# Waiting on GpSimd for the last four scatter-adds at the end of a fused cross-attention and mixture-of-experts kernel

## The chip, the cores and the metric

The kernel runs on one core of one Trainium2 chip. The metric is device time in microseconds (us): the time of one execution of the whole kernel. Three executions were timed before the change.

## The reference, cut to what matters

The kernel computes one decoder layer over 2048 rows of 256 numbers: self-attention, cross-attention over 1601 context rows, a dense feed-forward block, and then a mixture-of-experts block, which is the part that runs last:

```
router_logits = x @ wg.T                        # 8 experts
probs = softmax(router_logits)
topk_w, topk_idx = top_k(probs, 2)              # each row goes to two experts
topk_w = topk_w / sum(topk_w)
h1 = einsum('th,eih->tei', x, w1)
h3 = einsum('th,eih->tei', x, w3)
y = einsum('tei,ehi->teh', silu(h1) * h3, w2)
out = einsum('te,teh->th', expert_w, y)         # sum over the row's two experts
x = x + out
```

## The kernel before, in words

Five engines run a program each, written out by hand in one block: SyncE (SP), GpSimd (POOL), ScalarE (ACT), TensorE (PE) and VectorE (DVE). They order each other by counting semaphores alone. Up to about 350 us the kernel does the attention and dense parts; the rest is the expert part.

In the expert part the rows are sorted by expert into NJ = 39 tiles of 128 places. Tile n passes through a ring of RING = 4 buffers (slot n % 4):

- GpSimd gathers the tile's rows from the scratch tensor `hrow` by an indirect DMA (`gather`, line 899).
- PE multiplies with the expert's up-weights, ACT and DVE apply silu and the product (`e_sil`, `e_act`), SP turns the result by a DMA transpose (`act_turn`, line 658; for the last tile PE turns it instead), and PE multiplies with the down-weights.
- ACT or DVE scales the result by the gate and writes it to `ys` (`weighted`, DVE line 2208), which raises `e_y`.
- GpSimd adds the tile's 128 rows into the output tensor `out` in HBM by an indirect DMA with accumulation (`add`, line 925), called scatter-add below. When it has landed it raises the semaphore `e_add0` to `e_add3` of its slot by 16.

Each row of `out` gets two such additions, from two experts, so two scatter-adds that could meet the same row must not be in flight together. `add(n)` therefore waits on GpSimd for the landing of earlier scatter-adds (`add_done`, or a wait against a number read from a table), and issues a tiny multiplication into `gap` (line 923) ahead of the DMA. The waits of `add(38)`, the last one, are for scatter-adds 35, 36 and 37 or earlier ones, and then for `e_y` of tile 38.

GpSimd's program ends with `add(NJ - 1)`. SP's program ends with a wait for the landing of every scatter-add:

```
for s in range(RING):
    wait(sp, f"e_add{s}", 16 * len(range(s, NJ, RING)))
```

Of the kernel before, what the change touches and what calls it, by code (L numbers as in the profile page):

```python
# [61 lines left out]
NJ = (TOP * S + NE * (P - 1)) // P  # L62
# [7 lines left out]
RING, AHEAD, BEHIND = 4, 6, 3  # L70
# [8 lines left out]
def xattn_ffn_moe(nc, x, z, zT, w1, w2, wgT, we, b1, rows, out):  # L79
    with ExitStack() as ctx:  # L80
# [262 lines left out]
        def wait(eng, name, n):  # L343
            eng.wait_ge(sm[name], n)
# [119 lines left out]
        NG = len(GROUPS)  # L464
        LAG = 2
        LAST_OF = [max(n for n, (j, _) in enumerate(GROUPS) if j == b) for b in range(NB)]

        def width_of(parts):
            return sum((TB - t0) * P for _, t0, _ in parts)
# [209 lines left out]
        def _(pool):  # L679
# [148 lines left out]
            def weigh(j):  # L828

                b = slice(j * TB, (j + 1) * TB)  # L830
                wait(pool, "r_exp", j + 1)
                link(g.tensor_scalar(den[:], ex[:], 1.0, 1.0 / GS, ALU.add, ALU.mult))
                link(g.tensor_tensor(gf[:, :, 0], den[:], minus, ALU.pow))
                link(g.tensor_tensor(gf[:, :, 1], ex[:], gf[:, :, 0], ALU.mult))
                link(g.tensor_copy(vals[:, 1, b, :], gf))
                g.tensor_tensor(vals[:, 2, b, :], gf, vals[:, 1, b, :], ALU.subtract).then_inc(sm["r_val"], 1)
# [48 lines left out]
            def phase_of(n):  # L885
                return [p for p, (_, n0, n1) in enumerate(PHASES) if n0 <= n < n1][0]

            def rows_of(p):

                return PHASES[p][0] * TB * P if p < 2 else S + SPARE * P  # L890
# [11 lines left out]
            def add_done(n):  # L902
                wait(pool, f"e_add{n % RING}", 16 * (n // RING + 1))

            def add(n):

                p = phase_of(n)
                wait(pool, "x1_out", 16 * TB * PHASES[p][0])
                alone = n <= RING or n == PHASES[p][1]
                if n > 2:  # L910
                    add_done(n - 3)
                if n > 1 and (alone or n % RING == 1):
                    add_done(n - 2)
                if n and alone:
                    add_done(n - 1)
                if not alone:
                    if n == PHASES[p][1] + 1 or n == RING + 1:
                        wait(pool, "r_next", p + 1)
                    done = pool.value_load(before[0:1, n:n + 1], min_val=16, max_val=16 * NJ)
                    pool.wait_ge(sm[f"e_add{(n - 1) % RING}"], done)  # L920
                    if n % RING != 1:
                        pool.wait_ge(sm[f"e_add{(n - 2) % RING}"], done)
                    g.tensor_tensor(gap[:, n:n + 1], expo[:, 0:1], expo[:, 0:1], ALU.mult)
                wait(pool, "e_y", n + 1)
                g.indirect_dma_start(out[:rows_of(p), :], bass.IndirectOffsetOnAxis(ridx[:, n:n + 1], 0),  # L925
                                     ys[:, n % RING, :], None, compute_op=ALU.add
                                     ).then_inc(sm[f"e_add{n % RING}"], 16)
# [10 lines left out]
            for n in range(NJ):  # L938
# [7 lines left out]
                if n == LOGITS_AT - 2:  # L946
                    gates(NB - 1)
                    weigh(NB - 1)
            add(NJ - 1)

        @block.scalar
# [636 lines left out]
        def _(dve):  # L1589
# [397 lines left out]
            def tiles_hot(p):  # L1987

                _, n0, n1 = PHASES[p]
                k, n = pairs_of(p), n1 - n0  # L1990
                dve.wait_ge(sm["c_pv"], NT)
                link(v.scalar_tensor_tensor(hot_tiles(p), tkey[:, n0:n1].unsqueeze(1).broadcast_to([P, k, n]), float(P),
                                            keys.rearrange("p t c -> p (t c)")[:, :k].unsqueeze(2).broadcast_to([P, k, n]),
                                            ALU.mult, ALU.is_equal))
# [330 lines left out]
```

## Time and profile before

| what | value |
|---|---|
| device time, three runs | 554.15, 549.77, 547.66 us; median 549.77 us |
| span of the profiled execution | 546.3 us |
| busy share of the span: PE, DVE, ACT, POOL | 91%, 69%, 53%, 54% |
| instructions | 11105 |

The profiled execution has no device time of its own in the list. Its span, from the start of its first instruction to the end of its last, is 1.4 us under the fastest of the three runs and 3.5 us under their median. What lies between span and device time is outside the program's instructions. All rows below count time from the first instruction of that execution. A "q" behind an engine's name (POOLq, SPq) means its sequencer, the part that executes waits, branches and DRAINs and hands the rest to the engine. These do not count as busy.

### The profile page before, as it was taken

The page shows a single profiled execution, that of the slowest core. Times are in us where ns is not written, and L with a number is a line of the kernel's source. Part 1 is how long each engine was busy: PE and PEld are TensorE (multiplying, and loading weights), DVE is VectorE, ACT ScalarE, POOL GpSimd, SP SyncE. Part 2 cuts the span into 40 slices and gives each one's busy share as a digit, 9 for nine tenths or more (in the row PEclk, how much of TensorE's full clock was granted, in tenths as well). Part 3 has the DMA queues.
Part 4 walks back from the last instruction along what each step waited for, and adds up shares of the span by engine and source line. Part 5 has one row for each costly group of instructions (what it writes and reads, how often), then busy time and mean ns, then how long its engine had stood idle before and what let it go on. Part 6 is the DMA issues. An engine that isn't in the chain of part 4 may idle for free.

```text
span 546.3 us, 11105 instructions
## 1 busy us (share of the span) xinstructions
PE 499.1 (91%) x3721; PEld 329.5 (60%) x3721; DVE 377.8 (69%) x974; ACT 287.0 (53%) x588; POOL 295.8 (54%) x332
## 2 busy tenths in 40 slices
PE   3999999989999999799999988689997999999992
PEld 1676766655666675567565667444564656656661
DVE  5899886588777678868876887987866544444441
ACT  2747867564749446764457384474553333433430
POOL 3564121005553339735895759643647576777753
PEclk9999999999999999999999999999998999999997
DMA  8020624348895367863779553125796668887973
GB/s 273 8 71 26 193 69 131 92 83 144 154 162 133 97 112 142 172 155 90 117 181 193 155 92 108 54 71 109 139 161 93 94 123 133 133 134 127 135 109 39
DMA packets 135315, 65.62 MB, mean 120 GB/s; under 512 B 109757, under 2 KB 126590, under 8 KB 135262
## 3 DMA queue, kind: packets, MB, share of 16 engines
q1 hardware_dynamic: 127774, 54.69, 46.9%
q0 software_dynamic: 7488, 10.23, 12.4%
q8 instruction: 32, 0.52, 0.4%
q14 instruction: 21, 0.17, 0.1%
HBM read 28.19 MB, written 10.35 MB: 71 GB/s over the span
## 4 chain that ended last, share of the span: by engine, by line
PE 49%; DVE 15%; ACT 10%; POOL 9%; DMA 9%; issue 6%; POOLq 1%; SPq 0%; DVEq 0%; ACTq 0%
PE ps L1154 38%; DMA out<-y,qst 4%; ACT ps L971 3%; PE ps L1236 3%; PE ps L1238 3%; PE ps L1237 3%; POOL y L813 3%; ACT prob L970 3%; DVE cmax L1658 2%; DMA probT<-prob 2%; POOL y L846 1%; DMA y<-hrow,qst 1%; POOL rstd L806 1%; PE ps L1433 1%; DVE tT L1867 1%
## 5 line engine op out<-in xcount | busy, mean ns | idle before, releaser
L1154 PE MATMUL ps<-arena,probT 128*128 128x256 f16 (+2 forms) x1092 | 181.7, 319 | 5.6 <-DMA probT<-prob 3.1
L1154 PEld LDWEIGHTS ps<-arena,probT 128*128 128x128 f16 (+1 forms) x1092 | 104.9, 98 | 65.2 <-issue 11.8
L970 ACT ACTIVATE prob<-ps,nbias 128x512 f16<-128x512 f32 x64 | 39.0, 610 | 76.7 <-DVE nbias L1664 76.7
L925 POOL DMA_INDIRECT out<-y,qst x39 | 62.5, 1603 | 28.2 <-ACT y L1120 9.7
L1154 PE MATMUL ps<-arena,qT 128*128 128x512 f16 (+1 forms) x384 | 69.2, 332 | 3.1 <-DVE prob L1799 3.0
L2194 DVE SCALAR_TENSOR_TENSOR ps<-ps,w1m 128x512 f32<-128x512 f32 x39 | 27.3, 699 | 54.5 <-ACT w1m L1097 52.3
L1097 ACT ACTIVATE w1m<-ps 128x512 f32<-128x512 f32 x39 | 23.3, 597 | 76.3 <-PE ps L1154 61.5
L1154 PE MATMUL ps<-arena,tT 128*128 x468 | 57.9, 274 | 0.8 <-DVE tT L2289 0.6
L1154 PEld LDWEIGHTS ps<-arena,qT 128*128 128x128 f16 x384 | 32.5, 97 | 37.8 <-issue 4.2
L1799 DVE TENSOR_TENSOR prob<-ps,prob 128x512 f16<-128x512 f32 x64 | 36.3, 573 | 25.6 <-ACT ps L971 25.5
L1154 PE MATMUL ps<-tT 128*128 128x512 f16 (+3 forms) x240 | 51.8, 355 | 1.8 <-DVE tT L1626 1.8
L1154 PE MATMUL ps<-w2s,tT 128*128 128x256 f16 x384 | 48.2, 273 | 5.4 <-DVE tT L1867 5.1
L1154 PEld LDWEIGHTS ps<-arena,tT 128*128 128x128 f16 x468 | 44.1, 98 | 6.4 <-issue 1.3
L1154 PE MATMUL ps<-probT,w1m 128*128 128x512 f16 (+1 forms) x192 | 44.1, 326 | 3.5 <-DVE tT L1867 1.7
L899 POOL DMA_INDIRECT y<-hrow,qst x39 | 39.7, 1019 | 12.1 <-issue 11.2
L1154 PEld LDWEIGHTS ps<-w2s,tT 128*128 128x128 f16 x384 | 36.5, 98 | 15.9 <-issue 4.4
L989 ACT ACTIVATE probT<-ps,shift 128x512 f16<-128x512 f32 (+1 forms) x36 | 23.9, 664 | 31.9 <-PE ps L1154 21.0
L743 POOL TENSOR_TENSOR rstd<-veps,expo 128x1 f32<-128x1 f32 x16 | 10.0, 623 | 56.3 <-DVE veps L1693 56.3
L756 POOL TENSOR_TENSOR srstd<-sveps,expo 128x4 f32<-128x4 f32 x4 | 4.3, 1086 | 65.1 <-DVE sveps L1756 65.1
L1236 PE MATMUL ps<-arena,probT 128*128 128x257 f16 x136 | 37.2, 274 | 0.9 <-DVE probT L1726 0.5
L971 ACT ACTIVATE ps<-ps,nbias 128x512 f32<-128x512 f32 x64 | 37.5, 586 | 0.0
L1238 PE MATMUL ps<-arena,probT 128*128 128x257 f16 x136 | 37.1, 273 | 0.0
(214 smaller groups left out, 958.1 us busy)
## 6 DMA issues: line engine op xcount, KB each, us to landing
stage<-we_in SPq DMA_DIRECT2D x33, 256.0 KB, 3.2
prob<-we_in SPq DMA_DIRECT2D x15, 256.0 KB, 3.0
xin<-x_in SPq DMA_DIRECT2D x16, 128.0 KB, 2.8
out<-y SPq DMA_DIRECT2D x16, 128.0 KB
hrow<-tT SPq DMA_DIRECT2D x4, 512.0 KB, 4.7
y<-x_in SPq DMA_DIRECT2D x3, 512.0 KB, 6.5
stage<-z_in SPq DMA_DIRECT2D x4, 256.0 KB, 5.2
prob<-w_in SPq DMA_DIRECT2D x4, 256.0 KB, 3.0
```

The source lines that it names most:

```text
L813: g.tensor_scalar(blk(j)[:, m, :], blk(j)[:, m, :], mv4[:, m, 0:1], rstd4[:, m:m + 1], ALU.subtract, ALU.mult).then_inc(sm["n_nrm"], 1)
L899: g.indirect_dma_start(xg[:, n % RING, :], None, hrow[:rows_of(p), :], bass.IndirectOffsetOnAxis(ridx[:, n:n + 1], 0)).then_inc(sm[f"e_x{n ...
L925: g.indirect_dma_start(out[:rows_of(p), :], bass.IndirectOffsetOnAxis(ridx[:, n:n + 1], 0), ys[:, n % RING, :], None, compute_op=ALU.add). ...
L970: a.activation(row_cols(q, 0, c), ps[c][:, :w], ACT.Exp, bias=nbias[:, q, :], scale=SM)
L971: a.activation(ps[c][:, :w], ps[c][:, :w], ACT.Exp, bias=nbias[:, q, :], scale=SM, accum_out=esum[:, q, c:c + 1]).then_inc(sm["c_exp"], 1)
L989: a.activation(p16[:, s % 4, 0, :w], ps[s % 2][:, :w], ACT.Exp, bias=shift[:], scale=SM).then_inc(sm["s_exp"], 1)
L1097: a.activation(sil[:, q, :], ps[2 * q][:], ACT.Silu, scale=1.0 / WS).then_inc(sm["e_sil"], 1)
L1154: r = t.matmul(o, lhs(a), rhs(b), start=first and n == 0, stop=last and n == 2)
L1236: t.matmul(o[:, :D + 1], hi, yvh[:, kt, :D + 1], start=kt == 0, stop=False)
L1238: r = t.matmul(o[:, :D + 1], lo, yvh[:, kt, :D + 1], start=False, stop=last)
L1799: v.tensor_tensor(row_cols(q, 1, c), ps[c][:, :w], row_cols(q, 0, c), ALU.subtract).then_inc(sm["c_lo"], 1)
L2194: v.scalar_tensor_tensor(ps[2 * q + 1][:], ps[2 * q + 1][:], 1.0 / WS, sil[:, q, :], ALU.mult, ALU.mult).then_inc(sm["e_act"], 1)
```

## The change

Two lines are added behind the last `add` of GpSimd's program. NJ - RING is 35, so GpSimd waits for the landing of scatter-adds 35, 36, 37 and 38: `e_add3` at 144 and `e_add0`, `e_add1`, `e_add2` at 160. These are the four values that SP waits for already.

```
@@ -947,6 +947,8 @@
                     gates(NB - 1)
                     weigh(NB - 1)
             add(NJ - 1)
+            for n in range(NJ - RING, NJ):
+                add_done(n)
 
 
         @block.scalar
```

No computation and no DMA is added, removed or moved. The last rows of GpSimd's program before the change, from the last scatter-add to the branch into the end of the block (`qst` holds the table of row numbers, `ys` lies in `y`):

```order
L923 TENSOR_TENSOR gap<-expo 128x1 [waits e_add0]
L925 DMA out<-y,qst 2560x256 [waits e_y]
L919 TENSOR_LOAD qst [waits e_add3,x1_out]
L919 ISA x2
L923 TENSOR_TENSOR gap<-expo 128x1 [waits e_add0,e_add1]
L925 DMA out<-y,qst 2560x256 [waits e_y]
L80 UNCONDITIONAL_BRANCH
```

And after it, the same place of GpSimd's program:

```order
L919 TENSOR_LOAD qst [waits e_add3,x1_out]
L919 ISA x2
L923 TENSOR_TENSOR gap<-expo 128x1 [waits e_add0,e_add1]
L925 DMA out<-y,qst 2560x256 [waits e_y]
L80 UNCONDITIONAL_BRANCH [waits e_add1,e_add2,e_add0,e_add3]
```

Only the branch at the end differs: it now stands behind the four landings. The DRAIN of GpSimd comes after the branch in both. SP's program ends with the same waits in both:

```order
L565 DMA hrow<-tT 128x4x512 [waits m_hlo]
L658 DMA_TRANSPOSE tT<-prob 128x8x128 [waits e_alo,e_down] x29
L80 UNCONDITIONAL_BRANCH [waits e_add2,e_add3,e_add1,e_add0]
```

## Rows read from the trace of the kernel before

**Rows 1.** Windows view, last 14 us: busy time by engine, granted clock, DMA share, GB/s

```profile
core 0: us, PE busy (x) PEld busy (x) DVE busy (x) ACT busy (x) POOL busy (x), PEclk, DMA share, GB/s
532.00:539.60 7.60, 4.28 (x40) 3.17 (x37) 3.16 (x6) 1.32 (x3) 5.18 (x6) 0.99 0.55 60
539.60:541.90 2.30, 0.00 (x0) 0.00 (x0) 0.00 (x0) 0.00 (x0) 0.00 (x0) 0.50 0.55 57
541.90:546.30 4.40, 0.00 (x0) 0.00 (x0) 0.00 (x0) 0.00 (x0) 0.00 (x0) 0.50 0.01 2
```

**Rows 2.** Chain that ended last, stretch 526 to 547 us: start, length, what

```profile
526.28 6.54 PE ps L1154 x48
532.84 0.49 DVE y L2208
533.34 0.27 issue
533.61 3.47 DMA out<-y,qst
537.12 0.76 POOL gap L923
537.88 1.71 POOLq L80
```

**Rows 3.** Timeline of POOL, 525 to 547 us

```profile
525.79 0.18 POOL L923 TENSOR_TENSOR gap<-expo 128x1 f32<-128x1 f32 x1 [4.09 <-DMA out<-y,qst]
...
536.11 1.55 POOL L925 DMA_INDIRECT out<-y,qst  x1 [0.69 <-DVE y L2208]
537.12 0.76 POOL L923 TENSOR_TENSOR gap<-expo 128x1 f32<-128x1 f32 x1
538.04 1.55 POOL L925 DMA_INDIRECT out<-y,qst  x1 [0.16 <-issue]
```

**Rows 4.** Source view, line 80, the end of the block: ns min/median/max, first and last start

```profile
L80 POOLq EVENT_SEMAPHORE  x2: 17/17/17, 546.1 to 546.2; - x2
L80 ACTq DRAIN  x1: 626/626/626, 534.8 to 534.8; - x1
L80 PEldq DRAIN  x1: 638/638/638, 536.5 to 536.5; - x1
L80 DVEq DRAIN  x1: 524/524/524, 537.2 to 537.2; - x1
L80 POOLq DRAIN  x1: 8357/8357/8357, 537.7 to 537.7; - x1
L80 SPq COMPARE_BRANCH  x1: 41/41/41, 542.3 to 542.3; - x1
L80 SPq DRAIN  x1: 7/7/7, 542.5 to 542.5; - x1
```

**Rows 5.** Source view, line 344 (semaphore waits) on SP, 500 us to the end

```profile
L344 SPq EVENT_SEMAPHORE  x9: 17/17/28, 504.1 to 541.9; - x9
```

**Rows 6.** Waits of SP's queue, 515 us to the end: total, times, longest

```profile
SPq L344 <- DMA out<-y,qst: 11.7, 1, 11.7
...
SPq L80 <- PEq L80: 3.8, 1, 3.8
```

**Rows 7.** Source view, line 2318, the first instructions of the program

```profile
L2318 SPq DRAIN  x1: 7/7/7, 0.0 to 0.0; - x1
...
L2318 POOLq DRAIN  x1: 174/174/174, 0.4 to 0.4; - x1
L2318 POOL MEMSET const-uint8-127<- x1: 97/97/97, 0.4 to 0.4; 128x1 uint8 x1
```

More of the change, by code:

```diff
@@ L949, in _ @@
             add(NJ - 1)
+            for n in range(NJ - RING, NJ):
+                add_done(n)
         @block.scalar
```

## The prediction

> **What bounds the kernel now.** The change touches the last few microseconds alone, so I first split the end of the span by windows [rows 1]. Up to 539.6 us there is work on every engine. From there on no engine is busy. For 2.3 us the DMA engines still move data (share 0.55, 57 GB/s), and in the last 4.4 us they move almost nothing (share 0.01, 2 GB/s). So the program's last 4.4 us pass with neither computing nor transfer. The question is who holds the end of the span in that time.
>
> The chain that ended last [rows 2] goes PE, the scaling on DVE, a scatter-add that another one had to wait for (3.47 us), the `gap` multiplication, and then POOLq L80, GpSimd's sequencer at the end of the block. In that view its last piece is only 1.71 us long and begins at 537.88, which leaves the rest of the span unexplained. So I read the single instructions of line 80 [rows 4]. Five DRAINs stand there. ACT's, PE's and DVE's start between 534.8 and 537.2 and are done by 537.7. SP's starts at 542.5 and takes 7 ns. GpSimd's starts at 537.7 and takes 8357 ns, to 537.7 + 8.36 = 546.0 us. Its two semaphore instructions follow at 546.1 and 546.2, and the span ends at 546.3. **GpSimd's DRAIN ends last**, not SP's wait for the landings: SP reaches the meeting at 542.5 and sits there for 3.8 us [rows 6]. That wait is put down to PEq, but PE's DRAIN was over at 537.2; the engine that came last is GpSimd.
>
> What the DRAIN covers can be cut into three stretches:
> - 537.7 to 539.6: GpSimd's own last scatter-add, which starts at 538.04 and takes 1.55 us [rows 3]. The sequencer is ahead of its engine here, so the DRAIN is already begun while this instruction runs.
> - 539.6 to 541.9: the rows are landing. The last semaphore wait of SP is through at 541.9 [rows 5], so the last scatter-add takes 541.9 - 538.0 = 3.9 us from its start to its landing, near the 3.47 us that the chain shows for an earlier one [rows 2].
> - 541.9 to 546.0: 4.1 us in which the profile shows nothing that the DRAIN could wait for.
>
> From the end of the scatter-add's issue to the end of the DRAIN it is 546.0 - 539.6 = 6.4 us. From the end of the DRAIN to the end of the span it is 546.3 - 546.0 = 0.3 us, the meeting itself.
>
> **The change part by part.** It adds four waits ahead of GpSimd's branch and nothing else. On GpSimd only the branch, the DRAIN and the meeting are queued behind them, and who waits for these is all four other engines, which are idle by then. No gather or add is behind the waits, so nothing ahead of 539.6 us moves: the tiles, the transposes and the landings come as before. The waits themselves end at 541.9, as SP's equal ones do. The instructions cost 17 to 28 ns each [rows 5], and they lie in the time in which the rows land: nothing until 541.9. SP then needs from 541.9 to 542.5, 0.6 us, for what is left of its waits, its branch and the start of its DRAIN [rows 4, 5]. GpSimd's branch ran before under cover of its last scatter-add, and now it stands in the open as SP's does. So GpSimd's DRAIN should start at 541.9 + 0.6 = 542.5 instead of 537.7, 4.8 us later.
>
> All now hangs on how long a DRAIN of GpSimd takes that starts 0.6 us behind the last landing. No row of before shows that. The trace bounds it from both sides:
> - Short end: the DRAIN at the program's start takes 174 ns, and most of that is a MEMSET still running on the engine (97 ns, started beside it) [rows 7]. No scatter-add had gone out by then. With 0.17 us the span would end at 542.5 + 0.2 + 0.3 = 543.0: a change of -3.3 us.
> - Long end: the whole 8.36 us again, end at 542.5 + 8.4 + 0.3 = 551.2: +4.9 us. But 1.9 us of it (537.7 to 539.6) were the engine's own scatter-add, which is done by then; without them it is 6.4 us and an end at 549.2: +2.9 us.
> - Between them: if only the 4.1 us behind the landing are the DRAIN's own, they either run from the landing however the DRAIN starts (end as before, 0), or they start with the DRAIN (542.5 + 4.1 + 0.3 = 546.9, +0.6 us).
>
> I take the middle case, at the mean of its two ends, **+0.3 us**. The reason: the two DRAINs of GpSimd that the trace has differ in one thing above all, that the gathers and scatter-adds of 39 tiles stand between them, and the long one outlasts the last landing by 4.1 us. If it only waited for landings, as SP does, it would be over at 541.9 and not at 546.0. So it does something of its own that takes 4.1 us and comes with having issued such DMAs, and a wait for a semaphore on the sequencer does not do that work for it. Whether the work can run before the DRAIN asks for it is what splits 0 from +0.6.
>
> A rule of the Trainium skill speaks for another outcome. "VectorE: DVE Perf Modes", in the section "The DRAIN you can't avoid", says that the DRAINs which frame a kernel take a constant 12 ns or so on all five engines. The trace agrees for SP, at either end of the program (7 ns), and disagrees for GpSimd, with 174 and 8357 ns [rows 4, 7]. By that rule the whole length would be waiting, the DRAIN behind the new waits would be as short as SP's, and the end would come at 542.5 + 0.3 = 542.8, or -3.5 us. It is the first rival below, which is priced from the rows alone.
>
> **The sum.** Against the profiled execution: span 546.3 + 0.0 (everything ahead of 539.6) + 0.0 (the waits, under the landing) + 0.3 (the DRAIN) = 546.6 us. This execution lies 3.5 us under the median of the three runs, 549.77, so the forecast in device time is 549.8 + 0.3 = 550.1 us. The three runs are 6.5 us apart (1.2%), more than any case here is worth. About 1%, or 5.5 us, is what a measurement of this kernel can tell from no change.
>
> **The rivals.**
> - *The DRAIN was waiting for transfers, and finds none now.* Then it looks for finished transfers slowly or with long pauses while some are open, and the 4.1 us are that lateness. With nothing open it is as short as at the start of the program: -3.3 us, 546.5 us. For it: the 174 ns of [rows 7]. Against it: the DRAIN at the start had no DMA of GpSimd behind it at all, so it does not tell "all landed" from "none issued". Chance 0.25.
> - *The DRAIN costs a fixed time from its start on an idle engine.* Then 6.4 us that ran from 539.6, partly under the landing, now run from 542.5, wholly in the open: +2.9 us, 552.7 us. This is the rival on the other side: the change takes away an overlap. Its place is the DRAIN of GpSimd, its price 542.5 - 539.6 = 2.9 us, and it decides as soon as the DRAIN's own work does not depend on the landing. For it: nothing in the profile ties the DRAIN's end at 546.0 to the landing at 541.9 rather than to the issue's end at 539.6. Against it: only that a DRAIN of 6.4 us without any waiting is the longer guess. The extreme of it, 8.4 us from the start, gives +4.9 us, 554.7 us. Chance 0.2 and 0.03.
> - *The change does nothing that can be seen*, because SP waits for the same landings already and GpSimd would have met it at the block's end anyway. Without reading line 80 this is the natural reading; it gives 0 too, but it needs GpSimd's DRAIN to be off the path, and [rows 4] show that it is on it. Its time is part of the forecast's case.
>
> **How the numbers follow.** Forecast case, 0 to +0.6 us: 0.5 (its own range 549.8 to 550.4 us, before the scatter of runs). Short DRAIN: 0.25. Fixed DRAIN: 0.2, its extreme 0.03. The remaining 0.02 is for a change elsewhere in the program. The range runs from the short DRAIN's 546.5 less a little scatter, 545.8, to the fixed DRAIN's 552.7 and a little above, 553.0. No case is worth 1%: the largest likely ones are 3.3 / 549.8 = 0.6% down and 2.9 / 549.8 = 0.5% up. A change beyond 1% would come from a short or fixed DRAIN with the scatter of the runs on top of it. So: faster 0.08, same 0.86, slower 0.06.
>
> **What would show each step.** The windows up to 539.6 us should be as before, within a few tenths. Four waits of GpSimd at line 344, the last at 541.9 or 0.05 beside SP's. GpSimd's DRAIN starts near 542.5; if it starts much later, the branch costs more than SP's. The DRAIN's length tells the cases apart: 3.5 to 4.1 us is the forecast, under 0.3 us the short one, about 6.4 us the fixed one. SP's wait at line 80 is 3.8 us before; it should be 3.8 to 4.4 us in the forecast, 0.5 us with a short DRAIN, 6.7 us with a fixed one. The forecast is wrong if the gap from the last landing to the end of the span, 546.3 - 541.9 = 4.4 us before, changes by more than 1 us.

## The result, and the profile after

| | before | changed |
|---|---|---|
| median of 22 runs each, us | 549.87 (546.16 to 554.15) | 552.81 (548.97 to 558.11) |
| ratio, 95% interval | 1 | 1.0049 (1.0028 to 1.0070) |
| span of the profiled execution, us | 546.3 | 551.7 |

The ratios in this document leave out executions in a slower state (three of the 22 of the changed kernel, and some of kernels further down), the medians do not. The kernel became 0.5% slower: 0.0049 x 549.87 = 2.7 us, with an interval from 1.5 to 3.8 us. The forecast was +0.3 us, 550.1 us, with a range from 545.8 to 553.0 us and 0.86 for "within 1%". The time fell into the range, and the change is within 1%, but it is not the size of the forecast case. It is near the size of the rival that was given +2.9 us.

Windows of the changed kernel, cut at the same places of the program as [rows 1] (the end of the last scatter-add's issue, its landing, the end of the span), with the columns of that view:

```profile
535.00:542.60 7.60, 3.92 (x37) 2.89 (x34) 3.00 (x6) 1.19 (x2) 5.22 (x6) 1.00 0.53 62
542.60:544.80 2.20, 0.00 (x0) 0.00 (x0) 0.00 (x0) 0.00 (x0) 0.00 (x0) 0.76 0.57 60
544.80:551.70 6.90, 0.00 (x0) 0.00 (x0) 0.00 (x0) 0.00 (x0) 0.00 (x0) 0.50 0.00 1
```

The stretch in which the rows land is as long as before (2.2 against 2.3 us). The empty stretch behind it grew from 4.4 to 6.9 us, by 2.5 us. That is the change. Line 80 of the changed kernel answers to [rows 4]:

```profile
L80 PEldq DRAIN  x1: 558/558/558, 539.0 to 539.0; - x1
...
L80 POOLq COMPARE_BRANCH  x1: 41/41/41, 544.8 to 544.8; - x1
L80 POOLq DRAIN  x1: 6437/6437/6437, 545.0 to 545.0; - x1
L80 SPq COMPARE_BRANCH  x1: 41/41/41, 545.2 to 545.2; - x1
L80 SPq DRAIN  x1: 7/7/7, 545.3 to 545.3; - x1
```

GpSimd's DRAIN now starts at 545.0, behind the waits, and takes 6437 ns. Before it was on record for 8357 ns, but 1.9 us of those lay beside the last scatter-add's issue. The trace has 537.68 for its start there, so it ended at 537.68 + 8.36 = 546.04, and from the moment at which its engine was idle (539.60) it took 6.44 us. **The length is the same; only its start moved**, from the end of the issue to the landing. The last scatter-add in the timeline of the changed kernel, which answers to [rows 3]:

```profile
541.01 1.55 POOL L925 DMA_INDIRECT out<-y,qst  x1 [0.16 <-issue]
```

Its issue ends at 541.01 + 1.55 = 542.56, and the DRAIN starts 545.0 - 542.56 = 2.44 us later. From the end of that issue to the end of the span it is 551.7 - 542.56 = 9.1 us, against 546.3 - 539.59 = 6.7 us before. The waits of GpSimd (line 344) in the changed kernel, and those of SP's queue, which answer to [rows 6]:

```profile
L344 POOLq EVENT_SEMAPHORE  x4: 17/30/43, 537.4 to 544.7; - x4
```

```profile
SPq L80 <- PEq L80: 6.3, 1, 6.3
```

SP stands at the meeting for 6.3 us instead of 3.8. As before, PE is named and GpSimd is meant: PE's DRAIN was over at 539.6.

The two spans differ by 5.4 us, and 2.4 of it are explained. The rest was there before the changed place: PE's DRAIN stands at 539.0 us instead of 536.5. The added waits stand behind all work of GpSimd, so the change cannot reach that part, and executions of one and the same kernel differ by as much (the 22 runs of before lie 8 us apart). So from here on I compare stretches at the end of the program, which do not inherit that scatter, and use the ratios beside them.

### The profile page after: what moved, and what is told of

Same layout as the page of the kernel before. It is cut to its first block and busy times, and to the rows that moved or that the text cites. A ratio compares the mean times of both kernels' runs of the same rounds, so it can differ in the third digit from the quotient of the medians.

```text
span 551.7 us, 11108 instructions
## 1 busy us (share of the span) xinstructions
PE 500.1 (91%) x3721; PEld 330.8 (60%) x3721; DVE 383.4 (69%) x974; ACT 287.0 (52%) x588; POOL 297.7 (54%) x332
## 5 line engine op out<-in xcount | busy, mean ns | idle before, releaser
L1156 PE MATMUL ps<-arena,probT 128*128 128x256 f16 (+2 forms) x1092 | 179.8, 318 | 5.5 <-DMA probT<-prob 3.3
L1156 PE MATMUL ps<-probT,w1m 128*128 128x512 f16 (+1 forms) x192 | 45.8, 338 | 3.3 <-DVE tT L1869 1.7
L367 DVE SCALAR_TENSOR_TENSOR arena<-stage,arena 128x512 f16<-128x512 f32 (+2 forms) x37 | 38.8, 1053 | 5.1 <-ACT arena L363 5.0
L1238 PE MATMUL ps<-arena,probT 128*128 128x257 f16 x136 | 37.2, 274 | 0.5 <-DVE y L1738 0.3
```

The costliest lines, as they stand in the source:

```text
L367: nc.vector.scalar_tensor_tensor(piece[3], piece[1](q), piece[4], piece[2], ALU.mult, ALU.subtract).then_inc(sm["st_lo"], 1)
L1156: r = t.matmul(o, lhs(a), rhs(b), start=first and n == 0, stop=last and n == 2)
L1238: t.matmul(o[:, :D + 1], hi, yvh[:, kt, :D + 1], start=kt == 0, stop=False)
```

## The experiments

```
-        block = ctx.enter_context(nc.Block())
+        block = ctx.enter_context(nc.Block(no_gpsimd_drain=True))
```

> Edit: the kernel before, its block opened so that GpSimd executes no DRAIN at the end (the engines meet by semaphores alone). Theory F (a DRAIN of GpSimd behind indirect DMAs takes a fixed 6.44 us from the moment its engine is idle, and holds the end of the program): GpSimd waits at the meeting early, SP comes last, about 0.6 us behind the last landing, so from the last landing to the end of the span it is 0.8 to 1.1 us instead of 4.4, and the time falls by 3.3 to 3.6 us (0.6%). Rival L (the landing to HBM is what takes the time, and the DRAIN only shows it): the end stays 4 us behind the landing, 0.

> Edit: the changed kernel (GpSimd waits for the last four landings), and no DRAIN of GpSimd at the end of the block. Theory F: the added waits cost only because the DRAIN stands behind them; without it they end with SP's equal waits, so the time is that of e1_no_drain within 0.3 us: 3.3 to 3.6 us under before, some 6 us under the changed kernel. Rival W (the waits themselves, four polls of GpSimd's sequencer, cost the 2.7 us): this kernel is 2 to 3 us slower than e1_no_drain.

Measured: e1 0.9982 (0.9947 to 1.0018), e2 0.9960 (0.9925 to 0.9995). Line 80 of e1, then SP's semaphore waits in it:

```profile
L80 SPq COMPARE_BRANCH  x1: 41/41/41, 544.2 to 544.2; - x1
L80 SPq DRAIN  x1: 7/7/7, 544.4 to 544.4; - x1
```

```profile
L344 SPq EVENT_SEMAPHORE  x10: 17/17/28, 501.8 to 543.8; - x10
```

The last landing is through at 543.8 and the span ends at 544.7, 0.9 us later instead of 4.4. In e2 it is 537.9 and 538.8, 0.9 us as well. SP's waits in e2, and its line 80, which has GpSimd's branch behind its waits:

```profile
L344 SPq EVENT_SEMAPHORE  x9: 17/17/28, 500.0 to 537.9; - x9
```

```profile
L80 POOLq COMPARE_BRANCH  x1: 41/41/41, 538.0 to 538.0; - x1
L80 SPq COMPARE_BRANCH  x1: 41/41/41, 538.3 to 538.3; - x1
```

So rivals L and W fall: all but 0.9 us of the time behind the landing is the DRAIN's, and the four waits cost nothing at the end of the program when no DRAIN stands behind them. The time did not move to the start of the program either; GpSimd's DRAIN there (line 2318, [rows 7]) is as short in e1 as in the kernel before:

```profile
L2318 POOLq DRAIN  x1: 173/173/173, 0.4 to 0.4; - x1
```

Over whole runs, e1's interval reaches over 1 and does not show the gain by itself. The same edit once more, beside the changed kernel on one chip:

> Edit: as e1_no_drain, to narrow its interval beside the changed kernel on one chip. Theory N: 3.3 to 3.6 us faster than before (ratio 0.994), 5.9 to 6.3 us faster than the changed kernel.

> Edit: the changed kernel again. Theory N: the DRAIN of GpSimd 6.44 us from the end of the four waits; from the end of the last scatter-add's issue to the end of the span 9.1 us instead of 6.7, so 2.4 to 2.6 us (0.45%) slower than before.

Measured: 0.9926 (0.9899 to 0.9953) for e13, 1.0051 (1.0027 to 1.0074) for e14. In medians of the session: 544.17 us without the DRAIN, 548.60 us before, 551.36 us changed. The intervals of e1 and e13, which are the same kernel, only just overlap. The three ratios without the DRAIN (e1, e2, e13) lie 0.2, 0.4 and 0.7% under 1; the end of the program shows 4.4 - 0.9 = 3.5 us (0.6%). So the whole runs show that there is a gain, and the end of the program shows its size. In e14 the DRAIN is again at 6437 ns:

```profile
L80 POOLq DRAIN  x1: 6437/6437/6437, 542.9 to 542.9; - x1
```

### What the 6.44 us are

Two more DRAINs behind the waits of the changed kernel (this kernel and those of e5, e9 and e10 were run once each, so only their traces are read):

```
             for n in range(NJ - RING, NJ):
                 add_done(n)
+            g.drain()
+            g.drain()
```

> Edit: the changed kernel with two more DRAINs of GpSimd ahead of the one at the end of the block, behind the four waits: three in a row. Theory F, fixed per DRAIN: each takes 6.4 us, span 12.9 us longer than with one. Rival N (the 6.44 us are the bookkeeping of the indirect DMAs issued since the DRAIN before, 78 x 83 ns): the first takes 6.4 us, the second and third under 0.2 us, span as with one.

Measured, the source views of the two new lines and of line 80:

```profile
L952 POOLq DRAIN  x1: 6434/6434/6434, 540.1 to 540.1; - x1
```

```profile
L953 POOLq DRAIN  x1: 40/40/40, 546.6 to 546.6; - x1
```

```profile
L80 POOLq DRAIN  x1: 34/34/34, 546.7 to 546.7; - x1
```

Three DRAINs in a row take 6434, 40 and 34 ns. Theory F falls: a DRAIN has no fixed price, and what it costs comes from what went on since the DRAIN before. Now two DRAINs added to the kernel before in the middle of its program, where only four DMAs were issued:

```
+            wait(pool, "r_list", 1)
+            g.drain()
             gather(0)
             gather(1)
             gather(2)
             gather(3)
+            for n in range(RING):
+                wait(pool, f"e_x{n}", 16)
+            g.drain()
```

> Edit: the kernel before with two more DRAINs of GpSimd in the middle of the program: one just ahead of its first indirect DMA, one behind the landing of the first four gathers. Theory F, fixed per DRAIN once an indirect DMA went out: the first DRAIN is under 0.2 us, the second 6.4 us, the last at the end 6.4 us behind the engine's last work. Theory F0 (fixed for any DRAIN behind the start): the first takes 6.4 us too. Rival N (83 ns for each indirect DMA since the DRAIN before): second 0.33 us, last 74 x 83 ns = 6.1 us.

```profile
L930 POOLq DRAIN  x1: 1136/1136/1136, 353.0 to 353.0; - x1
```

```profile
L937 POOLq DRAIN  x1: 387/387/387, 364.0 to 364.0; - x1
```

```profile
L80 POOLq DRAIN  x1: 8643/8643/8643, 540.7 to 540.7; - x1
```

The timeline of GpSimd in this kernel has to be read beside them, since the first and the last record overlap the engine's own work:

```profile
353.05 1.03 POOL L806 TENSOR_TENSOR rstd<-veps,expo 128x4 f32<-128x4 f32 x1 [3.46 <-DVE veps L1608]
...
541.72 1.55 POOL L925 DMA_INDIRECT out<-y,qst  x1 [0.16 <-issue]
```

The first DRAIN ends at 354.1, 0.07 us behind the engine's multiplication (353.05 + 1.03): with no DMA issued it adds next to nothing to that work. The second takes 387 ns with four gathers behind it, all landed. The last ends at 540.7 + 8.64 = 549.4, and its engine was idle at 543.27, so it takes 6.11 us with 74 DMAs behind it, against 6.44 us with 78. N said 0.33 and 6.1 us. Next, whether the price is one of instructions or of rows. This is e5 with one more gather, of 32 rows, ahead of each of the first four (`e_half` is a semaphore added for them):

```
+                if n < RING:
+                    g.indirect_dma_start(xg[:32, n % RING, :], None, hrow[:rows_of(p), :],
+                                         bass.IndirectOffsetOnAxis(ridx[:32, n:n + 1], 0)).then_inc(sm["e_half"], 16)
+                    wait(pool, "e_half", 16 * (n + 1))
                 g.indirect_dma_start(xg[:, n % RING, :], None, hrow[:rows_of(p), :],
```

> Edit: e5_drain_early with one more gather of 32 rows ahead of each of the first four (they bring rows that the full gather brings again, and are waited for one by one). Theory N by instruction: the DRAIN behind them has 8 indirect DMAs to account for, 387 + 4 x 82 = 0.72 us, and the one at the end 6.11 us as there. By rows (128 rows = 82 ns): 387 + 4 x 21 = 0.47 us.

```profile
L941 POOLq DRAIN  x1: 708/708/708, 373.1 to 373.1; - x1
```

708 ns with eight gathers behind it, four of them of 32 rows: by instruction (by rows it would have been 0.47 us). From 387 and 708 ns each further DMA costs 80 ns; from 387 and 6437 ns it is (6437 - 387) / 74 = 82 ns. What remains is about 60 ns per DRAIN.

### Does a DRAIN wait for what is in flight?

In the kernel before, one DRAIN right behind the issue of the first four gathers:

```
             gather(2)
             gather(3)
+            g.drain()
```

> Edit: the kernel before with one DRAIN of GpSimd right behind the issue of the first four gathers, with no wait for their landing ahead of it. If a DRAIN waits for what is in flight, it ends with the last of the four landings or up to 0.4 us behind it, some 3 us behind the end of the fourth issue. If it only does its bookkeeping, it ends 0.4 us behind the end of the fourth issue.

```profile
L933 POOLq DRAIN  x1: 8306/8306/8306, 353.8 to 353.8; - x1
```

```profile
357.12 1.43 POOL L899 DMA_INDIRECT y<-hrow,qst  x1 [0.30 <-issue]
```

The fourth issue ends at 358.55 and the DRAIN at 353.8 + 8.3 = 362.1, 3.6 us later, where its bookkeeping for four is 0.4 us. The last of the four gathers' semaphore events is at 361.9. So a DRAIN does both: it takes its time for each DMA, and it does not end before the youngest has landed. (I call the first part its bookkeeping or account; the name is a guess at what is done, the time is measured.) In the kernel before, the 78 x 82 ns were the longer of the two, and the landing (2.3 us) lay wholly under them.

### The waits without the last scatter-add

The changed kernel, with this edit:

```
-            for n in range(NJ - RING, NJ):
+            for n in range(NJ - RING, NJ - 1):
                 add_done(n)
```

> Edit: the changed kernel, whose waits leave out the last scatter-add (35, 36 and 37 alone). Theory N (a DRAIN of GpSimd takes 82 ns for each of its indirect DMAs since the DRAIN before, 78 of them, and starts when its engine is idle and its waits are through): scatter-add 37 lands within 0.4 us of the end of the last issue, so the DRAIN starts at most 0.4 us later than in before and ends 6.4 to 6.9 us behind the last issue; the whole 2.7 us of the change go, time within 0.1% of before. Rival W (the waits themselves cost): three quarters of the loss stay, +2 us (0.4%).

```profile
L80 POOLq DRAIN  x1: 6437/6437/6437, 542.0 to 542.0; - x1
```

```profile
539.99 1.55 POOL L925 DMA_INDIRECT out<-y,qst  x1 [0.16 <-issue]
```

The DRAIN starts 0.5 us behind the end of the last issue (541.54; at most 0.4 was expected), not 2.4, and the span ends 7.2 us behind it (548.7), 0.5 us more than before. The ratio is 1.0018 (0.9978 to 1.0059), too wide to tell 0.1% from 0.4%; the stretch at the end tells it. Of the change's four waits, the one for the last scatter-add carries 2.0 of the 2.4 us.

### Paying earlier

If the account is kept since the last DRAIN, an earlier DRAIN should shorten the last one. First, in the kernel before, one in every scatter-add from tile 17 on:

```
+                if n > E_LOOP:
+                    g.drain()
                 wait(pool, "e_y", n + 1)
```

> Edit: the kernel before with a DRAIN of GpSimd in each scatter-add from tile 17 on, ahead of its wait for e_y. Theory N with a DRAIN that waits for nothing in flight: each of the 21 later ones takes 0.04 + 2 x 0.082 = 0.2 us, the first (tile 17) some 40 x 0.082 = 3.3 us, and the last one at the block's end 0.12 us; the end of the span is then set by SP's wait for the landing, 3.4 us under before, less what the DRAINs cost in the loop (0 to 4 us). Theory N with a DRAIN that waits for landings too: each one in the loop lasts until the youngest gather or scatter-add has landed, 1 to 3 us, GpSimd falls behind and the kernel is 10 to 50 us slower; the last DRAIN ends with the last landing. Rival F (a fixed 6.4 us per DRAIN behind indirect DMAs): 22 DRAINs, over 50 us slower, and the last one is still 6.4 us long.

Measured: 1.0754 (1.0688 to 1.0821). The source view of the DRAINs in the loop, the same view for the first of them alone (460 to 469 us), and the longest waits of the engines from 470 us on:

```profile
L925 POOLq DRAIN  x22: 364/3384/4144, 465.2 to 578.8; - x22
```

```profile
L925 POOLq DRAIN  x1: 3577/3577/3577, 465.2 to 465.2; - x1
```

```profile
DVE y L2210 <- DMA out<-y,qst: 61.5, 16, 4.6
ACT w1m L1099 <- PE ps L1156: 43.3, 16, 4.1
```

There are 22 of them. In the first, at 465.2 us, the engine was long idle and 43 DMAs were to account for; it took 3.58 us, as N says (26 gathers and 17 scatter-adds; 43 x 0.082 + 0.06 = 3.59). Most of the others are counted in microseconds though they have one or two DMAs behind them, and e10 gives the reason: a DRAIN waits for landings. Scatter-adds come late, DVE waits 61.5 us for them, and the kernel is 41 us slower. It is the second reading of N that came out. Then a single one, in the scatter-add of tile 33, where GpSimd had stood idle for 4.09 us [rows 3], without and with the change:

```
+                if n == 33:
+                    g.drain()
                 if n > 2:
                     add_done(n - 3)
```

> Edit: the kernel before with one more DRAIN of GpSimd, in the scatter-add of tile 33, ahead of its waits for earlier landings, where GpSimd stood idle for 4.09 us in before. Theory N: it accounts for 39 gathers and 33 scatter-adds, 72 x 0.082 + 0.04 = 5.9 us, of which 4.1 us are the old idle time, so scatter-add 33 is about 2 us late and 34 and 35 too, 36 to 38 are not. The DRAIN at the end has 6 scatter-adds left, 0.5 us, and ends with the last landing, 2.4 us behind the end of the last issue instead of 6.4: about 3.2 to 3.5 us faster than before (0.6%), from the last landing to the end of the span 0.8 to 1.1 us. Rival F (any last DRAIN behind indirect DMAs costs 6.4 us): slower by up to 2 us, last DRAIN 6.4 us.

> Edit: e11_one_drain_in_slack and the change together. Theory N: with 6 scatter-adds left to account for, the DRAIN behind the four waits takes 6 x 0.082 + 0.04 = 0.53 us instead of 6.44; it starts 0.3 us behind the last landing and ends 0.8 us behind it, so the change costs 0.2 us here instead of 2.5. Rival: whatever the change costs in the kernel as it was (2.5 us from the last issue to the end of the span) it costs here too.

Measured: e11 0.9994 (0.9969 to 1.0020), e12 1.0021 (0.9994 to 1.0048). The added DRAIN, line 80 and the timeline of e11, then line 80 and the timeline of e12:

```profile
L911 POOLq DRAIN  x1: 9234/9234/9234, 522.5 to 522.5; - x1
```

```profile
L80 PEldq DRAIN  x1: 637/637/637, 538.8 to 538.8; - x1
...
L80 POOLq DRAIN  x1: 5042/5042/5042, 543.4 to 543.4; - x1
L80 SPq DRAIN  x1: 7/7/7, 548.8 to 548.8; - x1
```

```profile
523.55 1.55 POOL L927 DMA_INDIRECT out<-y,qst  x1 [0.16 <-issue]
532.43 0.18 POOL L925 TENSOR_TENSOR gap<-expo 128x1 f32<-128x1 f32 x1 [7.32 <-issue]
...
541.77 0.18 POOL L925 TENSOR_TENSOR gap<-expo 128x1 f32<-128x1 f32 x1 [1.31 <-DMA out<-y,qst]
542.43 1.55 POOL L927 DMA_INDIRECT out<-y,qst  x1 [0.47 <-issue]
...
544.37 1.55 POOL L927 DMA_INDIRECT out<-y,qst  x1 [0.16 <-issue]
```

```profile
L80 POOLq DRAIN  x1: 552/552/552, 547.6 to 547.6; - x1
```

```profile
543.47 1.55 POOL L927 DMA_INDIRECT out<-y,qst  x1 [0.16 <-issue]
```

At the end of the program N holds. In e11 the last DRAIN ends with the landing, and from the landing (548.2) to the end of the span (549.0) it is 0.8 us. In e12 the DRAIN behind the four waits takes 552 ns for six scatter-adds (0.53 was expected), and its span ends 548.4 - 545.02 = 3.4 us behind the end of the last issue, against 3.1 us in e11. **With a short account the change costs 0.3 us at the end of the program instead of 2.4**; the two ratios over whole runs are too wide to tell this.

In e11's loop the expectation failed twice. The added DRAIN was to take 5.9 us for its 72 DMAs. It ends at 522.5 + 9.23 = 531.7, and its engine was idle at 523.55 + 1.55 = 525.10, so it took 6.6 us; the one of e12, read in the same way, took 6.1. Why two DRAINs in the middle of the program come out longer than the price of 82 ns was not tried. And the idle time in front of scatter-add 33 grew to 7.32 us, the ones behind it did not catch up, since they wait for each other's landings, and the last one starts 544.37 - 538.8 = 5.6 us behind PE's DRAIN instead of 538.04 - 536.5 = 1.5. In these two executions that is 4 us, as much as the 3.5 us gained. It need not all be the DRAIN's: in e10, which has none there, the last scatter-add comes as late, 544.68 - 539.2 = 5.5 us behind PE's DRAIN:

```profile
544.68 1.55 POOL L925 DMA_INDIRECT out<-y,qst  x1 [0.16 <-issue]
```

```profile
L80 PEldq DRAIN  x1: 638/638/638, 539.2 to 539.2; - x1
```

The ratio of e11 over whole runs, 0.9994 where 0.994 was expected, shows that the gain is lost. So this version is no gain, and leaving GpSimd's DRAIN out is the one that beats both kernels.

## Why the prediction was right or wrong

- **GpSimd's DRAIN holds the end of the span:** right, and it carried the whole case. e1, e2 and e13 take it away, and SP comes last, 0.9 us behind the landing.
- **The waits cost nothing themselves:** right (e2 against e1). **They delay the DRAIN by the landing:** right; it starts at 545.0, 0.3 us behind its last wait (544.7), where I had taken 0.6 from SP. SP's branch follows its last wait by 0.4 us (545.2 against 544.8), GpSimd's by 0.1.
- **The length of the delayed DRAIN, the step that failed:** I took "the 4.1 us behind the landing are the DRAIN's own", 4.1 us or less, for +0.3 us. They are no quantity of their own. The DRAIN is 6.44 us from the engine's idle moment, and 4.1 is what is left of it when the landing is through. So neither end of my case, 0 or +0.6 us, came. My reason was half right: the work is the DRAIN's own and comes with having issued indirect DMAs. But if it comes from the issues and not from the landing, it starts when the engine is idle, and that is the argument for 6.44, not 4.1. I weighed against the 6.4 us case only that it was "the longer guess", which is no evidence. Its term, 2.9 us, came out as 2.4, mostly because the branch was quicker than SP's.
- **"The work can run before the DRAIN asks for it"**, which was to split 0 from +0.6: it does not. In e4 the account is settled by the first DRAIN only, although it started 0.1 us behind the last wait and all of the earlier DMAs had long landed.
- **The short DRAIN (0.25):** wrong. It would need a DRAIN to be short once its DMAs have landed, and in e4 it took 6434 ns there. The Trainium skill ("VectorE: DVE Perf Modes", "The DRAIN you can't avoid") gives about 12 ns for the DRAINs that the runtime puts around a kernel. The DRAIN here belongs to the kernel's own block, as e1 shows, so that figure did not have to hold for it: SP's 7 ns are near it, GpSimd's 6437 ns are not.
- **Size and chances:** +2.7 us measured, within the range and within 1%, as given at 0.86. That the range held was the rival's doing and not the forecast's: it reached up to 553.0 only because the fixed DRAIN (0.2) was counted in. By the prediction's own sign the forecast case was wrong, since the gap from the last landing to the end of the span changed by 2.5 us and not by less than 1. The rival had the right size for a reason that is only half right: the DRAIN runs on its own from the idle engine, but its time is not fixed (e4). It is 6.44 us because 78 indirect DMAs lay behind it.

## What to carry to other kernels

A DRAIN of GpSimd is priced by the indirect DMAs issued since its last DRAIN, here about 82 ns each, and it runs from the moment at which that engine is idle. Let it overlap the last landing: a wait on GpSimd ahead of it puts the two in series, while the same wait on another engine is free. Where another engine already waits for every landing, as SP does here, the block can end without GpSimd's DRAIN; this was shown only for a block with nothing behind it. When an interval in a profile is cut in pieces, ask of each piece whether it has a start of its own: a remainder behind some event is not evidence of work that begins there.

## What the runs showed of the hardware that I had not expected

A DRAIN of GpSimd took about 60 ns plus 80 to 82 ns for each indirect DMA issued since the DRAIN before it, landed or not, of 32 rows or of 128: 387 ns for 4, 552 for 6, 708 for 8, 3.58 us for 43, 6.11 us for 74, 6.44 us for 78, and 34 to 40 ns for none. Three do not fit: 6.6 and 6.1 us for 72 in the middle of the program (e11, e12; 5.96 by this price), and 364 ns for a single one that had just landed (0.14 by this price), the shortest of e8. It also waited for the youngest DMA in flight (it ended 0.2 us behind the landing in e10). Its record in the trace begins while its engine still works, so its length there (8357 ns before the change, 6437 after it) cannot be compared without the engine's last instruction. Why an entry takes 82 ns was not tried, nor whether plain DMAs of GpSimd cost the same.
